# A mixer step of 3328 TensorE instructions, the loop's head at slot 148 of 256, and the third u score block ahead of the key projection's first half

## The reference, cut

```python
xx = xprev - x
mix = jnp.tanh((x + xx * time_maa_x) @ time_maa_w1.T).reshape(B, T, 4, -1)
xrg, xwa, xk, xv = x[None] + xx[None] * (time_maa + einsum(mix, time_maa_w2))
r, k, v = xrg @ receptance.T, xk @ key_w.T, xv @ value.T
...
def step(S, inp):                      # for each time step, per head, S is 32 x 32
    r_, w_, k_, v_, kk_, b_ = inp
    sab = jnp.einsum('bhvk,bhk->bhv', S, kk_)
    S = S * jnp.exp(w_)[:, :, None, :] + sab[..., None] * b_[:, :, None, :] + v_[..., None] * k_[:, :, None, :]
    return (S, jnp.einsum('bhvk,bhk->bhv', S, r_))
```

## Time and profile before

| what | value |
|---|---|
| time, median of 3 runs | 5907.34 us (5901.49 to 5909.01) |
| time of the profiled execution | 5900.49 us |
| its span, first to last instruction | 5898.6 us |
| mean granted TensorE clock | 0.972 |
| busy: TensorE matmul / VectorE / ScalarE / GpSimd | 92% / 63% / 34% / 24% |
| the loop's two turns, from 232.60 to 3619.60 us | 3387.0 us |

### The profile page before, as it was taken

How to read it: one execution, slowest core, us unless ns; L and a number is a source line. 1 busy time by engine, 2 the same in 40 slices (tenths; PEclk the granted TensorE clock), 3 DMA queues, 4 the chain that set the end, 5 groups by cost and what they waited for, 6 DMA issues and landing times. The chain is left out here.

```text
span 5898.6 us, 243936 instructions
## 1 busy us (share of the span) xinstructions
PE 5437.2 (92%) x110664; PEld 3805.1 (65%) x110664; DVE 3741.3 (63%) x9004; ACT 2014.6 (34%) x3659; POOL 1396.8 (24%) x1156
## 2 busy tenths in 40 slices
PE   6999999999989999899999999975999999999998
PEld 6777777777777777777777777752444444444443
DVE  6788888788888788878888888845232232232310
ACT  4444444444444444444444444420000000000000
POOL 1222222222222222222222222212022022121220
PEclk9999999999999999999999999987999999999999
DMA  1001000010100000010000000003112112112110
GB/s 62 23 18 25 18 21 22 18 25 18 25 18 23 21 20 24 18 25 18 23 20 23 21 20 23 16 16 97 61 50 93 50 52 102 50 52 99 39 64 14
DMA packets 108638, 211.07 MB, mean 36 GB/s; under 512 B 25553, under 2 KB 26705, under 8 KB 107089
## 3 DMA queue, kind: packets, MB, share of 16 engines
q1 hardware_dynamic: 92240, 144.91, 8.4%
q0 software_dynamic: 15360, 50.48, 2.6%
HBM read 144.60 MB, written 50.72 MB: 33 GB/s over the span
## 5 line engine op out<-in xcount | busy, mean ns | idle before, releaser
L392 DVE COPY_PREDICATED time_raw<-time_known,w_bank 128x96 f32<-128x96 int32 (+6 forms) x3072 | 816.7, 274 | 214.0 <-PE w_bank L1043 128.5
L1862 PE MATMUL moe_bank<-moe_w,moe_hidden 128*128 128x512 f32 x2048 | 930.4, 597 | 0.0
L1849 PE MATMUL moe_bank<-moe_hT,moe_w 128*128 128x512 f32 x2048 | 924.3, 594 | 1.5 <-DVE moe_hT L1743 1.5
L1764 ACT ACTIVATE moe_hidden<-moe_bank,moe_b 128x512 f32<-128x512 f32 x256 | 175.9, 687 | 1635.3 <-PE moe_bank L1849 1635.3
L1849 PEld LDWEIGHTS moe_bank<-moe_hT,moe_w 128*128 128x128 f32 x2048 | 386.5, 190 | 471.7 <-issue 469.8
L1862 PEld LDWEIGHTS moe_bank<-moe_w,moe_hidden 128*128 128x128 f32 x2048 | 379.8, 190 | 429.7 <-issue 428.2
L909 POOL TENSOR_TENSOR time_grow<-time_eye,time_grow 128x512 f32<-128x512 f32 x256 | 371.7, 1452 | 1131.6 <-DVE time_grow L418 1131.6
L1028 PE MATMUL w_bank<-time_ew,time_grow 32*32 32x64 f32 x32768 | 403.8, 218 | 160.4 <-issue 143.6
L1028 PEld LDWEIGHTS w_bank<-time_ew,time_grow 32*32 32x32 f32 x32768 | 350.7, 104 | 199.4 <-issue 157.2
L1043 PE MATMUL w_bank<-time_keys,time_queries_u 32*32 32x160 f32 x8192 | 362.5, 309 | 31.5 <-issue 20.3
L1743 DVE COPY moe_hT<-moe_bank 128x512 f32<-128x512 f32 x64 | 44.2, 691 | 501.0 <-PE moe_bank L1834 501.0
(11 more groups left out here) (226 smaller groups left out, 9421.5 us busy)
## 6 DMA issues: line engine op xcount, KB each, us to landing
moe_w<-in_w SPq DMA_DIRECT2D x64, 1024.0 KB, 7.4
mid_xn<-time_xn_rows SPq DMA_DIRECT2D x128, 129.0 KB, 2.5
time_x_rows<-in_x SPq DMA_DIRECT2D x128, 128.0 KB, 2.7
time_base<-in_x SPq DMA_DIRECT2D x128, 128.0 KB, 3.0
mid_acc<-time_mixed SPq DMA_DIRECT2D x128, 128.0 KB, 2.4
mid_scores<-time_rated SPq DMA_DIRECT2D x128, 2.0 KB, 1.7
moe_b<-in_b SPq DMA_DIRECT2D x8, 256.0 KB, 12.8
time_key_w<-in_w_key_w SPq DMA_DIRECT2D x1, 1024.0 KB, 5.3
```

Source lines behind the costliest of these rows:

```text
L392: e.copy_predicated(by_raw[:, "uy".index(q), n0:n1, :, 0:8 * j + 8], known[:, "uy".index(q), :, :, mine].to_broadcast([P, n1 - n0, 2, 8 * ...
L1764: e.activation(hidden[now % 4][:, :], up[now % 3][:, :], ACT.Gelu_apprx_tanh, bias=b1[:, x * FC + k:x * FC + k + 1]).then_inc(act.sem, act ...
L1849: got = e.matmul(up[now % 3][:, :], w1[:, g * F + k * P:g * F + (k + 1) * P], hT[x % 2][:, g * CAP + half * HALF:g * CAP + (half + 1) * HA ...
L1862: got = e.matmul(down[t][:, :], hidden[now % 4][:, t * P:(t + 1) * P], tile(w2, k), start=k == 0, stop=k == FC - 1)
```

## The change

It drops 17 instructions that only wait from each full step of TensorE, which leaves 3328. It moves `score("u", 2)` from behind S16 to between `low("low_k", 2)` and `key_of(0, 2)`. And it places the loop's head on TensorE at instruction 148 of a block of 256. In the changed order S2 is instructions 443 to 698 of a step (its wait ahead), S8 1121 to 1376, low_k 1378 to 1393, u2 1394 to 1441, the first key half 1442 to 1473, and S16 1475 to 1730.

```diff
--- before.py
+++ after.py
@@ -18,6 +18,7 @@
 ROW = C + 4
 SETS = 4
 LONG = 28
+PAGE = 256
 
 
 class Steps:
@@ -273,7 +274,7 @@
             "B.rk B.qu C.b1 C.b2 C.b4 C.faded0 C.b8 B.qy B.e1 B.us A.lt C.faded1 B.ys").split()
         PE_STEPS = (
             "A.x C.S1 A.scored D.centre A.mix B.value D.var A.delta C.S2 D.gate A.gate1 B.bonus C.S4 A.low_wa B.u0 B.u1 "
-            "C.S8 A.low_k C.S16 B.u2 A.key B.u3 A.decay B.u4 B.u5 A.low2 B.y0 B.y1 A.sums C.z0 B.y2 B.y3 C.u0 C.y0 D.out "
+            "C.S8 A.low_k B.u2 C.S16 A.key B.u3 A.decay B.u4 B.u5 A.low2 B.y0 B.y1 A.sums C.z0 B.y2 B.y3 C.u0 C.y0 D.out "
             "B.y5 B.y4 C.z1 C.u1 A.recept C.y1").split()
         BANK = Banks(psum, [
             ("x", 0, act, "A.x_tile"), ("delta1", 0, dve, "A.lerp13"), ("low_wa", 0, act, "A.hid_a"), ("mk", 0, act, "A.thmk"),
@@ -1008,11 +1009,9 @@
             def inverse_stage(k, half):
 
                 if half == 0:
-                    clear(e, f"S{k}")
-                    clear(e, f"S{k}+")
                     if k == 1:
-                        if "C.rows1" in dve.was:
-                            e.wait_ge(dve.old, dve.ago("C.rows1"))
+                        clear(e, "S1")
+                        clear(e, "S1+")
                         e.wait_ge(pool.old, pool.ago("B.e1"))
                     else:
                         e.wait_ge(act.sem, act[f"C.S{k // 2}"])
@@ -1035,8 +1034,9 @@
 
                 for m in which:
                     clear(e, f"{q}{m}")
-                    e.wait_ge(dve.sem, dve["B.kk0"])
-                    e.wait_ge(pool.sem, pool[f"B.q{q}"])
+                    if m == 0:
+                        e.wait_ge(dve.sem, dve["B.kk0"])
+                        e.wait_ge(pool.sem, pool[f"B.q{q}"])
                     n0, n1 = UNITS[m]
                     for n in range(n0, n1):
                         for h in range(HG):
@@ -1181,9 +1181,7 @@
                 mm.then_inc(pe.sem, pe.step("A.decay"))
 
             def low_second():
-                for name in ("mk", "aaa", "ma"):
-                    clear(e, name)
-                e.wait_ge(act.sem, act["A.k"])
+                e.wait_ge(act.sem, act["A.tail"])
                 for g in range(G):
                     for i, name in enumerate(("key", "mk", "aaa", "ma")):
                         mm = e.matmul(BANK[name][:, g * P:(g + 1) * P], wt["low_w2"][head(i), g * P:(g + 1) * P], hid4[head(i), :],
@@ -1245,13 +1243,14 @@
                 inverse_stage(8, 1)
             if A:
                 low("low_k", 2)
+            if Bs:
+                score("u", 2)
+            if A:
                 clear(e, "key")
                 key_of(0, 2)
             if Cs:
                 inverse_stage(16, 0)
                 inverse_stage(16, 1)
-            if Bs:
-                score("u", 2)
             if A:
                 key_of(2, 4).then_inc(pe.sem, pe.step("A.key"))
             if Bs:
@@ -1329,6 +1328,7 @@
         step(-1, 3, "NABC")
         step(0, 4, "NABCD")
         turns = (tiles - 8) // LONG
+        nc.tensor.addr_align(PAGE, offset=148)
         with nc.Fori(0, turns) as part_of_tiles:
             for i in range(LONG):
                 step(part_of_tiles * LONG + (i + 1), SETS + 1 + i, "NABCD")
```

## The result

The kernel after takes 5822.01 us (median of 4 runs, 5811.03 to 5827.01), the one before 5908.18 in the same comparison: a ratio of 0.9856, 95% interval 0.9841 to 0.9870. That is 86 us less, where 14 were forecast, and it lies outside the range.

What follows compares the result with a forecast made beforehand. TensorE was taken to be bound by stops at fetched-block crossings and the halved clock behind them. From 61.37: -0.47 -1.0 +0.2 +0.15 -0.05, and 0.07 for the turn back; 14 us less in all, 5893 us, range 5835 to 5940.

Steps and rivals of the forecast that it cites:

- What bounds the kernel: TensorE stops where it crosses from one fetched 256-instruction block to the next; stops shown were 1.64 to 2.04 us.
- The 17 waits: Dropped waits in the inverse, score blocks and second low-rank product: 0 to 0.17 us a step, 0.05 us off taken.
- u2: Third u score block moved ahead of key half and S16: costs 0 to 0.3 us a step more, 0.15 taken.
- Its cover: The low_k stop hides u2's wait for DVE's masks of u0; without a stop u2 would wait 0.4 us.
- the S16 crossing: Block 1387 to 1643 now holds 3.9 us against 3.69, so a stop in S16 of 0 to 0.8, 0.2 taken.
- The S2 stop: Crossing 619, 40 matmuls before S2's end: stop of 1.58 to 1.91 us kept, halved clock in 2 of 6.
- The low_k stop: Stop at 1387 inside low_k of 1.65 us, 0.47 less than the four steps' S8 stops, mean 2.12.
- the sum from four steps of before: Four steps with first crossing at 103 or 104, mean 61.37 us, changed by the terms to 60.2 us a step.
- its clock term: Halved clock behind the low_k stop in 1 of 3 steps where it was 4 in 4: 1.0 us less.
- (a): Rival: the low_k stop halves the clock nearly every step; slower, 5950 us; chance 0.22.
- p: Share of steps with a halved clock behind low_k's stop; a step is 59.8 + 1.5 p us, a loss from 0.5.
- (b): Rival: crossings hardly matter or the alignment isn't as said; a stop still moves each step; 5907 within 10; chance 0.13.

Runs made afterwards that it cites:

- offset 118: The kernel after with the loop's head at instruction 118 of a block of 256 in place of 148: 5864.2 us.
- offset 199: The kernel after with the loop's head at instruction 199 of a block of 256 in place of 148: 5841.3 us.
- u2 back: The kernel after, head still at 148, with the third u score block back in its old place behind S16: 5942.7 us.
- offset 159: The kernel after with the loop's head at instruction 159 of a block of 256 in place of 148: 5845.0 us.
- offset 236: The kernel after with the loop's head at 236 in place of 148: 5781.1 us, repeated 5789.1; with u2 in its old place 5771.1, repeated 5774.4.

## Why the prediction was wrong, point by point

**What bounds the kernel: right.** Idle time was where blocks meet, at the instructions named, in all 56 steps, and it moved with every offset.

**The 17 waits: small by themselves, as forecast.** Their worth is that 3328 is a multiple of 256: with them kept, and the other two parts made, a step is 0.11 us shorter than before. At one place the idle time prices them: ahead of the second low-rank product it is 12.5 and 12.7 us in the loop of the two kernels that have the waits, and 10.1 in each kernel without them, 0.04 us a step. What they cost elsewhere is open: with u2 in one place, steps without a halved clock are 0.39 and 0.54 us shorter in busy time without the waits (54.33 for 54.72, 54.54 for 55.08), but the placing of the head alone moves that figure from 54.54 to 55.31. Whether dropping any other 17 instructions would do wasn't tried.

**u2: a term mis-sized.** Its cover held: in the kernel after, the masks of u0 end 2.5 us of idle time in the whole run. Where the stop is gone (offset 118) it waits 0.36 us, against the 0.4 worked out. Its price is 0.21 to 0.28 us a step where 0.15 was taken. That the move frees the S16 crossing was forecast, for the wrong reason: the block's 3.9 us were set against 3.69, while the runs point to a request behind S16's wait. 0.2 us of stop was taken and none came.

**The S2 stop: right in place and size** (1.58 to 1.91 forecast, 1.73 on average measured), and right that the request hangs behind a wait ahead of the delta group. The wait's releaser was probably named wrong. The kernel waits there for the mix and for ScalarE's copy of the value rows too, whose bank the fourth delta needs. In the step shown (the row below) that copy ends at 1427.56, 1.25 us after the mix, and the delta group begins at 1427.82.

```profile
1426.97 0.59 ACT L727 COPY time_v<-w_bank 128x512 f32<-128x512 f32 x1 [0.67 <-PE w_bank L996]
```

With offset 199 S2 resumes 3.63 us after that copy's end (3.48 to 4.03 in 55 steps) and 4.89 after the mix's; the first is S16's 3.65. In the kernel after it is 4.19 us (3.95 to 4.50). There the 66th instruction behind the crossing lies 53 behind the wait, with offset 199 it lies 2 behind it, which may be the difference; it isn't shown.

**The low_k stop: in the right place, mis-sized.** 1.46 us where 1.65 was taken. From crossing 1131 to the resumption at 1387 it is 3.58 us on average, 3.20 to 4.13: 3.69 was one pair's value, and some blocks come sooner.

**The step that failed is the sum from four steps of before, its clock term above all.** The forecast took a halved clock with one low_k stop in 3, and kept S2's 2 in 6. Measured: 9 of 56 behind low_k's stop and 7 of 56 behind S2's. The four steps' 61.37 us are 56.67 busy and 4.70 idle; a step after is 55.07 busy and 4.02 idle.
- Busy time fell by 1.60 us, where the forecast let 1.0 go for the clock and added 0.15 for u2. The clock's share is 1.42: steps at full clock take 54.72 us before, so 1.95 of the four's 56.67 are the clock's, and of after's 55.07, 0.53 (54.54 at full clock). The other 0.18 is work that went faster, u2's price included, where 0.15 more was forecast.
- Idle time fell by 0.67 us, where the forecast let 0.47 - 0.2 + 0.05 - 0.07 = 0.25 go: low_k's stop is 0.19 shorter than taken, and S16's 0.2 never came.

The two errors, 0.75 and 0.42, make the 1.17 us (60.27 less 59.10) by which the step was overestimated, 65 us in 56 steps. Outside the loop the forecast had 2 us of gain and the trace 4 of loss, which takes 6 off. The remaining 13 of the 72 us between 14 and 86 lie in no term: the forecast was worked out for the profiled run, and the two profiled runs are 73 us apart (5900.5 and 5827.0), the medians 86.

Why are there fewer halvings? The length of the stops is a part of it. In the kernel after none of the 46 stops under 1.55 us is followed by a halved clock, of the 66 longer ones 16 are; and 29 of low_k's 56 turned out under 1.55. But the loop before has 64 stops of 1.55 us or more, as many as after, and 32 of them are followed by a halved clock: 17 of 22 from 2.0 us on and 15 of 42 below, against 4 of 10 and 12 of 56 after. So at equal length a stop halves the clock less often in the kernel after, and why stays open. The same S2 stop (1.73 us after, 1.66 with u2 back) was followed by it in 7 of 56 steps and in 16.

The Trainium skill (Runtime: NRT & Kernel Launch, Instruction fetch mechanics) says that the cost of crossing a 16 KiB boundary is "mostly hidden". The trace after has 179 us of stops at two crossings of the loop, so it does not hold here.

**The rivals.** (a) is real (21 of 56 at offset 159, 9 of 56 here), but p = 0.16 is far under the 0.5 from which it makes a loss. (b) fell: the stops stand still. (c)'s 5770 is nearer to the 5822 measured than the forecast's 5893 is, but by luck, for S2's stop stayed; at offset 236, where it does go, the time is 5771 to 5789, close to its 5770.

## What to carry to other kernels

Where a loop of short matmuls is long against the fetched block, count instructions: a body that is a multiple of 256 instructions fixes the crossings, and then their place must be chosen by trying, since here the same work in the same order took from 5781 to 5961 us by that place alone. Look at each crossing for two things: how many us of work the block holds, and whether a wait that ends late stands in the first 70 or so instructions behind it. When a forecast rests on a few analog stretches of a wandering pattern, split them into idle and busy time first, and sum each for itself.

## What the runs showed of the hardware

- TensorE behaves as if the next block were asked for some 64 to 70 instructions behind a crossing, and not while the sequencer stands at a wait short of that. The request itself is in no trace; the stops are: a stop in 55 of 56 steps with the wait 64 behind, in 29 of 56 at 68, in 50 of 56 at 70 (if that wait is the one), in none at 83 and 87. TensorE goes on 3.5 to 4.1 us after such a wait's releaser ends (S16 with u2 back, S2 at offset 199), 3.95 to 4.50 us at S2 in the kernel after.
- Stops have steps in their length: 1.49, 1.77 and 2.04 us at S2, some 0.27 us apart.
- The clock after a stop is not set by its length alone: 2.04 us gave 0.65 once and 1.00 in the next step. With u2 back at offset 148, 19 low_k stops of 1.55 us or more, followed at once by the key half, were not followed by a halved clock once; in the kernel after, with u2 between, 9 of 27 were.
- Over the 56 steps after, busy time grows by 0.47 us for each us at half clock. With 64.8 us in 18 stretches that is some 1.7 us a stretch, an estimate, near the 1.5 that was taken.
